# Gated cross-attention with routed experts: one copy for a head's six outputs, the exponentials' bias on GpSimd, and the row maxima one more unit ahead

## The chip, the cores and the metric

The kernel runs on one core of a Trainium2 chip. The metric is the device time of one launch in microseconds. Before the change it is 1069.77 us (median of three runs, 1069.75 to 1071.2).

## What is computed

The reference is one transformer block on 800 tokens of width 512. It has a cross-attention of 16 heads of width 32 with quantised queries, keys, values and probabilities, a gated residual, and a mixture of experts behind it. The change touches only the attention:

```python
q, k = _fq_sym(q, axis=-1), _fq_sym(k, axis=-1)      # integers times a step per row
v = _fq_sym(v, axis=2)                               # step per column
attn = softmax(einsum('bhqd,bhkd->bhqk', q, k))      # 2888 keys
attn = _fq_unsigned(attn, axis=-1)                   # x / (row max / 255), rounded, 0..255
out  = einsum('bhqk,bhkd->bhqd', attn, v)            # then the output projection
```

A row's largest probability becomes 255. So the kernel writes exp(step * s - step * max(s) + ln 255) straight as an unsigned byte, and needs the row's maximum before the first exponential.

## The kernel before, in words

The attention loop works on NTILE = 100 units. A unit is 128 query rows of one head against all 2888 keys. The 800 tokens make T = 7 row tiles, and the seventh holds 32 tokens. A head has six units of whole tiles, and four heads share a seventh, the tail unit, so each of the NG = 4 groups has GT = 25 units, the tail unit last. `tile_place(n)` gives group, head and tile of a unit.

The scores of a unit are six blocks of 481 or 482 columns (`BLOCK_W`). TensorE makes them twice, because PSUM does not hold them until the maximum is known.

- For the maximum (`for_max`, L587, products at L577): four spans per unit (`MAX_SPANS`), of two blocks, one, two and one. The spans of two blocks always use banks 0 and 1, and the others bank 2 (`MAX_BANK`). Span c waits until VectorE has reduced span c-2 (`pe.wait_ge(s_max, c - 1)`).
- For the exponentials (`for_exp`, L599, same L577): three spans of two blocks (`EXP_SPANS`) in two alternating pairs of banks. Span c waits for exponential c-2.

Each engine runs its own list in order:

- VectorE (L1056 to L1078): maximum 0 of unit n (L1052), the row maximum of unit n-1 over its four spans (L1062), maximum 1 of n, the bias of unit n-1 (L1072), maxima 2 and 3 of n. At n = 1 it also quantises the last group of values (L978 to L988). Before the loop it makes `neg_tail_step` (L1044).
- ScalarE (L884 to L891): three exponentials of unit n (L866), each followed by reading its sum; then `keep_output(n - 3)`, which copies a finished 128x32 output out of PSUM (L875). For a tail unit these are four copies (L879).
- SyncE (L449 to L460): a DMA transpose of the unit's bytes (`transpose_p`, L446). It waits for the unit's three exponentials and, as there are only NT8 = 2 target buffers, for the widening of unit n-2. Between them stand the transposing loads of keys (L401), four for each head.
- GpSimd (L1345 to L1350): widens the transposed bytes of unit n to bf16 (L1349, a 128x3072 cast) once the transpose has landed.
- TensorE (`weigh_values`, L608, L619): 24 products of the widened probabilities with the values into `OUT_BANK`, each unit behind the copy of the one before (`s_ao`).

TensorE's order is written out by hand and is what ties the rest together (L631 to L645). In pass n it issues, in turn: exponential span 0 of unit n-1, maximum span 2 of n, exponential span 1 of n-1, maximum span 3 of n, the value products of n-4, maximum span 0 of n+1, exponential span 2 of n-1, maximum span 1 of n+1.

`exp_bias`, `row_max` and `span_max` have two buffers each, by the parity of the unit.

## Time and profile before

| what | value |
|---|---|
| median of three runs | 1069.77 us |
| the profiled execution, its time | 1069.22 us |
| its span, first to last instruction | 1067.7 us (1.5 us lie around it) |
| attention loop, first to last maximum | 217 to 594 us |
| PE, DVE, ACT, POOL busy over the span | 93%, 60%, 47%, 40% |
| mean granted TensorE clock | 0.971 of full speed |

PE is TensorE, PEld its weight loads, DVE is VectorE, ACT is ScalarE, POOL is GpSimd, SP is SyncE. A busy time is a sum over instructions. A row of the time line merges instructions of one kind; "x2" in it means two instructions, and what stands in brackets is the idle time before the row and what ended it. The time of a merged row runs from its first start to its last end.

### The profile page before, as it was taken

The page shows a single profiled execution, that of the slowest core. Times are in us where ns is not written, and L with a number is a line of the kernel's source. Part 1 is how long each engine was busy: PE and PEld are TensorE (multiplying, and loading weights), DVE is VectorE, ACT ScalarE, POOL GpSimd, SP SyncE. Part 2 cuts the span into 40 slices and gives each one's busy share as a digit, 9 for nine tenths or more (in the row PEclk, how much of TensorE's full clock was granted, in tenths as well). Part 3 has the DMA queues.
Part 4 walks back from the last instruction along what each step waited for, and adds up shares of the span by engine and source line. Part 5 has one row for each costly group of instructions (what it writes and reads, how often), then busy time and mean ns, then how long its engine had stood idle before and what let it go on. Part 6 is the DMA issues. An engine that isn't in the chain of part 4 may idle for free.

```text
span 1067.7 us, 16598 instructions
## 1 busy us (share of the span) xinstructions
PE 988.1 (93%) x5718; PEld 500.9 (47%) x5719; DVE 644.1 (60%) x1140; ACT 499.1 (47%) x1072; POOL 431.7 (40%) x293
## 2 busy tenths in 40 slices
PE   5999999879999999999999699999999999999993
PEld 2334444324444444444444356555665665565551
DVE  4895766599999999999999545821111111111156
ACT  2022222259999999999999532111221122122110
POOL 1043333217777777777677500171111111111065
PEclk9999999989999999999999788999999999999996
DMA  9954655688888888888786444154445655653155
GB/s 321 226 200 178 208 192 202 195 152 146 139 139 130 141 140 143 142 138 133 133 136 111 68 168 168 39 199 141 167 176 183 230 191 188 236 181 114 49 166 152
DMA packets 268272, 172.45 MB, mean 162 GB/s; under 512 B 239344, under 2 KB 239344, under 8 KB 265904
## 3 DMA queue, kind: packets, MB, share of 16 engines
q1 hardware_dynamic: 258512, 140.14, 54.2%
q0 software_dynamic: 9696, 31.47, 8.7%
q8 instruction: 39, 0.64, 0.2%
q14 instruction: 25, 0.20, 0.1%
HBM read 68.67 MB, written 44.63 MB: 106 GB/s over the span
## 4 chain that ended last, share of the span: by engine, by line
PE 56%; DVE 16%; POOL 11%; ACT 8%; issue 6%; DMA 3%; SPq 0%; POOLq 0%; DVEq 0%; ACTq 0%
PE ps L692 17%; PE ps L712 10%; POOL arena_a L1349 8%; PE ps L577 8%; ACT arena_a L866 7%; PE ps L560 6%; PE ps L537 5%; DVE span_max L1052 4%; PE ps L619 3%; POOL expert_in L1358 2%; PE ps L662 2%; PE ps L722 1%; DVE v_q L1273 1%; PE ps L703 1%; DVE proj_i L1011 1%
## 5 line engine op out<-in xcount | busy, mean ns | idle before, releaser
L1052 DVE TENSOR_REDUCE span_max<-ps 128x1 f32<-128x481 f32 (+2 forms) x400 | 351.4, 904 | 17.5 <-PE ps L577 8.4
L866 ACT ACTIVATE arena_a<-ps,exp_bias,q_step 128x962 uint8<-128x962 f32 (+1 forms) x288 | 329.7, 1156 | 20.7 <-DVE exp_bias L1072 11.2
L1349 POOL CAST arena_a<-arena_a 128x3072 bf16<-128x3072 uint8 x100 | 273.7, 2747 | 129.3 <-DMA arena_a<-arena_a 119.0
L577 PE MATMUL ps<-arena_a,q_t 128*128 128x481 bf16 (+1 forms) x864 | 224.4, 372 | 18.6 <-DVE span_max L1052 7.0
L692 PE MATMUL ps<-arena_a,xt 128*128 x544 | 172.2, 459 | 1.7 <-issue 1.7
L1211 DVE TENSOR_TENSOR proj_d<-ps,proj_f 128x352 f32<-128x352 f32 x48 | 25.1, 524 | 205.5 <-ACT proj_f L901 205.4
L712 PE MATMUL ps<-arena_a,proj_r 128*128 (+3 forms) x288 | 134.1, 602 | 0.7 <-ACT proj_r L907 0.7
L907 ACT COPY proj_r<-ps 128x128 f32<-128x128 f32 x144 | 28.4, 270 | 227.1 <-PE ps L703 227.1
L577 PEld LDWEIGHTS ps<-arena_a,q_t 128*128 128x128 bf16 x864 | 61.5, 97 | 148.9 <-ACT arena_a L866 73.0
L692 PEld LDWEIGHTS ps<-arena_a,xt 128*128 128x128 f32 x544 | 100.4, 190 | 61.2 <-issue 17.9
L619 PEld LDWEIGHTS ps<-v_q,arena_a 128*128 128x128 bf16 x2400 | 77.0, 97 | 31.2 <-POOL arena_a L1349 12.8
L560 PE MATMUL ps<-arena_a 128*128 128x512 f32 (+1 forms) x192 | 84.5, 586 | 6.3 <-ACT xt L829 4.0
L619 PE MATMUL ps<-v_q,arena_a 128*128 128x32 bf16 (+1 forms) x2400 | 79.8, 179 | 7.6 <-POOL arena_a L1349 5.7
L537 PE MATMUL ps<-arena_a 128*128 128x512 f32 x184 | 82.2, 592 | 0.0
L1364 POOL DMA_DIRECT2D xt<-expert_in x36 | 19.4, 539 | 147.8 <-PE ps L722 145.8
L577 PE MATMUL ps<-arena_b,q_t 128*128 128x481 bf16 (+1 forms) x288 | 75.1, 370 | 3.9 <-ACT arena_a L866 0.3
L712 PEld LDWEIGHTS ps<-arena_a,proj_r 128*128 128x128 f32 (+1 forms) x288 | 52.9, 194 | 50.9 <-issue 47.0
L692 PE MATMUL ps<-arena_a,q_t 128*128 128x352 f32 x224 | 73.2, 472 | 0.0
L841 ACT CAST parts<-proj_d 128x512 bf16<-128x512 f32 x23 | 14.2, 618 | 115.8 <-DVE proj_d L1022 115.8
L1229 DVE COPY xt<-ps 128x512 f32<-128x512 f32 x34 | 23.5, 691 | 69.0 <-PE ps L712 69.0
L1358 POOL DMA_INDIRECT expert_in<-arena_b,slot_i x28 | 26.8, 959 | 89.6 <-DVE slot_i L1190 81.4
L560 PEld LDWEIGHTS ps<-arena_a 128*128 128x128 f32 x192 | 37.4, 197 | 51.8 <-issue 43.2
(166 smaller groups left out, 909.6 us busy)
## 6 DMA issues: line engine op xcount, KB each, us to landing
arena_a<-in_w_up SPq DMA_DIRECT2D x18, 1408.0 KB, 6.4
arena_a<-in_w_down SPq DMA_DIRECT2D x18, 768.0 KB, 8.4
key_parts<-parts SPq DMA_DIRECT2D x23, 512.0 KB, 2.6
expert_in<-xt SPq DMA_DIRECT2D x42, 256.0 KB, 3.0
xt<-expert_in POOLq DMA_DIRECT2D x36, 256.0 KB, 3.0
expert_out<-xt POOLq DMA_DIRECT2D x34, 256.0 KB, 2.3
arena_a<-in_ctx_t SPq DMA_DIRECT2D x3, 1536.0 KB, 13.6
expert_out<-xt SPq DMA_DIRECT2D x17, 256.0 KB, 3.1
```

What stands on the lines that cost most here:

```text
L537: last = mm(ps[:, 2 + j % 2, :], src, w_qkv[:, 0 if j < T else 1, k, :], start=(k == 0), stop=(k == DC - 1))
L560: last = mm(ps[:, 4 + v % 2, 0:w], w_qkv[:, 2, k, g * P:(g + 1) * P], ctx_sb[:, k, c * BANK:c * BANK + w], start=(k == 0), stop=(k == DC - 1))
L577: last = mm(ps[:, bank + b, 0:w], q_t[:, head, t * P:(t + 1) * P], k_t[head % NK][:, a:a + w], start=True, stop=True)
L619: last = mm(ps[:, OUT_BANK, 0:w], p_t[n % NPT][:, c, :], v_q[:, c, a:a + w], start=(c == 0), stop=(c == 2 * PC - 1))
L692: last = mm(ps[:, 1 + 2 * q + w, 0:INTER], src(k), arena_a[:, bass.ds(col + (w * DC + k) * INTER, INTER)], start=(k == 0), stop=(k == DC - 1))
L712: last = mm(ps[:, 6 + q, :], h_t[0:IW[c], q, c * P:(c + 1) * P], arena_a[0:IW[c], bass.ds(col + UPC + c * D, D)], start=(c == 0), stop=(c ...
L866: nc.scalar.activation(halves[:, :, a:a + w], ps[:, bank:bank + 2, 0:w], ACT.Exp, bias=exp_bias[:, n % 2:n % 2 + 1], scale=step_of, accum_ ...
L907: last = nc.scalar.copy(h_t[0:IW[c], q, c * P:(c + 1) * P], ps[0:IW[c], 5, c * P:(c + 1) * P])
L1052: v.tensor_reduce(span_max[:, n % 2, j:j + 1], ps[:, bank:bank + len(blocks), 0:w], AX.XY, ALU.max).then_inc(s_max, 1)
L1211: v.tensor_tensor(h_mul[:, q, 0:INTER], ps[:, 2 + 2 * q, 0:INTER], h_act[:, q, 0:INTER], ALU.mult).then_inc(s_hm, 1)
L1349: p.tensor_copy(p_t[n % NPT].rearrange("p c q -> p (c q)").rearrange("p (j i) -> p j i", j=2), pt_u8[n % NT8].rearrange("p (i j) -> p j i" ...
L1358: p.indirect_dma_start(out=expert_in, out_offset=bass.IndirectOffsetOnAxis(ap=slot_i[0:rows, j, t:t + 1], axis=0), in_=xn[0:rows, t, :], i ...
```

## The change

Four things are changed in the attention loop.

1. The outputs of the six whole units of a head go side by side into one PSUM bank (`OUT_RUNS` lists units whose outputs go together), and ScalarE copies them in one instruction of 128x192 after the sixth. A tail unit keeps its four copies. TensorE waits for a copy only at the first unit of a run.
2. The bias of the exponentials is made by GpSimd instead of VectorE. GpSimd makes those of units 0, 1 and 2 before its first widening, and then that of unit n+3 right behind the widening of unit n. A new semaphore says when `neg_tail_step` is there.
3. VectorE's row maximum of unit n-1 now waits for the bias of unit n-3, which frees its buffer. Its waits for the row maximum and for the exponentials move to GpSimd.
4. TensorE's order has the exponentials of unit n-2 and the value products of n-5 beside the maxima of n and n+1. The loop has one pass more.

```diff
+        OUT_RUNS, RUN_OF = [], []
+        for n in range(NTILE):
+            g, head, t = tile_place(n)
+            own = ("tail", g) if head is None else ("head", head)
+            if not OUT_RUNS or OUT_RUNS[-1][0] != own:
+                OUT_RUNS.append((own, []))
+            OUT_RUNS[-1][1].append(n)
+            RUN_OF.append(len(OUT_RUNS) - 1)
...
                 pe.wait_ge(s_conv, n + 1)
-                if n:
-                    pe.wait_ge(s_ao, n)
+                run = OUT_RUNS[RUN_OF[n]][1]
+                if n == run[0] and n:
+                    pe.wait_ge(s_ao, RUN_OF[n])
+                at = (n - run[0]) * HD
                 for c in range(2 * PC):
-                    last = mm(ps[:, OUT_BANK, 0:w], p_t[n % NPT][:, c, :], v_q[:, c, a:a + w],
+                    last = mm(ps[:, OUT_BANK, at:at + w], p_t[n % NPT][:, c, :], v_q[:, c, a:a + w],
...
-            for n in range(NTILE + 4):
-                if n >= 2:
-                    for_exp(n - 1, 0)
+            for n in range(NTILE + 5):
+                if n >= 3:
+                    for_exp(n - 2, 0)
                 for_max(n, 2)
-                if n >= 2:
-                    for_exp(n - 1, 1)
+                if n >= 3:
+                    for_exp(n - 2, 1)
                 for_max(n, 3)
...
-                weigh_values(n - 4)
+                weigh_values(n - 5)
                 for_max(n + 1, 0)
-                for_exp(n - 1, 2)
+                for_exp(n - 2, 2)
                 for_max(n + 1, 1)
...
             def keep_output(n):
 
+                kind, run = OUT_RUNS[RUN_OF[n]]
+                if n != run[-1]:
+                    return
                 g, head, t = tile_place(n)
                 act.wait_ge(s_av, n + 1)
-                if head is not None:
-                    last = nc.scalar.copy(attn[:, t, head * HD:(head + 1) * HD], ps[:, OUT_BANK, 0:HD])
+                src = ps[:, OUT_BANK, 0:len(run) * HD]
+                if kind[0] == "head":
+                    last = nc.scalar.copy(attn[:, 0:T - 1, head * HD:(head + 1) * HD],
+                                          src.rearrange("p (t d) -> p t d", d=HD))
...
                 if n:
                     dve.wait_ge(s_max, NM * n)
+                    if n >= 3:
+                        dve.wait_ge(s_bias, n - 2)
                     v.tensor_reduce(row_max[:, prev % 2:prev % 2 + 1], span_max[:, prev % 2, :], AX.X, ALU.max
                                     ).then_inc(s_row, 1)
                 if n < NTILE:
                     maximum(n, 1)
-                if n:
-                    g, head, t = tile_place(prev)
-                    neg_step = neg_tail_step[:, g:g + 1] if head is None else neg_q_step[:, head, t:t + 1]
-                    dve.wait_ge(s_row, n)
-                    if n >= 3:
-                        dve.wait_ge(s_exp, NE * (prev - 1))
-                    v.tensor_scalar(exp_bias[:, prev % 2:prev % 2 + 1], row_max[:, prev % 2:prev % 2 + 1],
-                                    neg_step, LOG255, ALU.mult, ALU.add).then_inc(s_bias, 1)
...
+            def bound_exps(n):
+
+                g, head, t = tile_place(n)
+                neg_step = neg_tail_step[:, g:g + 1] if head is None else neg_q_step[:, head, t:t + 1]
+                if n == 0:
+                    pool.wait_ge(s_ntail, 1)
+                pool.wait_ge(s_row, n + 1)
+                if n >= 2:
+                    pool.wait_ge(s_exp, NE * (n - 1))
+                p.tensor_scalar(exp_bias[:, n % 2:n % 2 + 1], row_max[:, n % 2:n % 2 + 1],
+                                neg_step, LOG255, ALU.mult, ALU.add).then_inc(s_bias, 1)
+
+            AHEAD = 3
+            for n in range(AHEAD):
+                bound_exps(n)
             for n in range(NTILE):
                 pool.wait_ge(s_pt[n % NT8], 16 * (n // NT8 + 1))
                 if n >= NPT:
                     pool.wait_ge(s_av, n - NPT + 1)
                 p.tensor_copy(p_t[n % NPT].rearrange("p c q -> p (c q)").rearrange("p (j i) -> p j i", j=2),
                               pt_u8[n % NT8].rearrange("p (i j) -> p j i", j=2)).then_inc(s_conv, 1)
+                if n + AHEAD < NTILE:
+                    bound_exps(n + AHEAD)
```

## Rows read from the trace of the kernel before

**Rows 1.** The page: costliest groups; form, count, busy us, mean ns, idle before.
```profile
L1349 POOL CAST arena_a<-arena_a 128x3072 bf16<-128x3072 uint8 x100 | 273.7, 2747 | 129.3 <-DMA arena_a<-arena_a 119.0
L866 ACT ACTIVATE arena_a<-ps,exp_bias,q_step 128x962 uint8<-128x962 f32 (+1 forms) x288 | 329.7, 1156 | 20.7 <-DVE exp_bias L1072 11.2
```

**Rows 2.** Stretch: PE, PEld, DVE, ACT, POOL busy (x); clock, DMA share, GB/s.
```profile
240.00:312.00 72.00, 69.16 (x727) 29.98 (x727) 69.52 (x118) 70.01 (x139) 52.87 (x21) 1.00 0.89 144
```

**Rows 3.** Time line of VectorE early in the loop, before values and copies run.
```profile
229.56 3.00 DVE L1052 TENSOR_REDUCE span_max<-ps 128x1 f32<-128x962 f32 x3
232.47 0.15 DVE L1062 TENSOR_REDUCE row_max<-span_max 128x1 f32<-128x4 f32 x1
```

**Rows 4.** Time line of VectorE, 280.3 to 289 us.
```profile
279.31 1.16 DVE L1052 TENSOR_REDUCE span_max<-ps 128x1 f32<-128x964 f32 x1
280.39 0.15 DVE L1062 TENSOR_REDUCE row_max<-span_max 128x1 f32<-128x4 f32 x1
281.02 0.20 DVE L1072 TENSOR_SCALAR exp_bias<-row_max,neg_q_step 128x1 f32<-128x1 f32 x1
281.15 3.00 DVE L1052 TENSOR_REDUCE span_max<-ps 128x1 f32<-128x962 f32 x3
284.06 0.14 DVE L1062 TENSOR_REDUCE row_max<-span_max 128x1 f32<-128x4 f32 x1
```

**Rows 5.** Time line of the weight loads of TensorE, 280.3 to 284.9 us.
```profile
280.52 0.11 PEld L577 LDWEIGHTS ps<-arena_a,q_t 128*128 128x128 bf16 x2 [0.40 <-DVE span_max L1052]
281.14 0.32 PEld L577 LDWEIGHTS ps<-arena_a,q_t 128*128 128x128 bf16 x3 [0.51 <-ACT arena_a L866]
281.57 0.85 PEld L619 LDWEIGHTS ps<-v_q,arena_a 128*128 128x128 bf16 x24
282.36 0.73 PEld L577 LDWEIGHTS ps<-arena_a,q_t 128*128 128x128 bf16 x5
```

**Rows 6.** Time line of ScalarE, 228 to 242 and 280.3 to 284.9 us.
```profile
237.01 1.16 ACT L866 ACTIVATE arena_a<-ps,exp_bias,q_step 128x964 uint8<-128x964 f32 x1 [0.16 <-DVE exp_bias L1072]
...
281.26 1.16 ACT L866 ACTIVATE arena_a<-ps,exp_bias,q_step 128x964 uint8<-128x964 f32 x1
283.53 1.16 ACT L866 ACTIVATE arena_a<-ps,exp_bias,q_step 128x962 uint8<-128x962 f32 x1
```

**Rows 7.** SyncE's transposes of the bytes (L446): from issue to landing.
```profile
DMA to landing us min/median/max: 3.6/4.0/5.4
```

**Rows 8.** Time lines of GpSimd and ScalarE around three casts.
```profile
238.05 2.75 POOL L1349 CAST arena_a<-arena_a 128x3072 bf16<-128x3072 uint8 x1 [4.14 <-DMA arena_a<-arena_a]
240.69 1.16 ACT L866 ACTIVATE arena_a<-ps,exp_bias,q_step 128x964 uint8<-128x964 f32 x1
...
361.54 2.75 POOL L1349 CAST arena_a<-arena_a 128x3072 bf16<-128x3072 uint8 x1 [1.56 <-DMA arena_a<-arena_a]
363.64 1.16 ACT L866 ACTIVATE arena_a<-ps,exp_bias,q_step 128x964 uint8<-128x964 f32 x1
...
589.83 5.44 POOL L1349 CAST arena_a<-arena_a 128x3072 bf16<-128x3072 uint8 x2 [2.16 <-DMA arena_a<-arena_a]
```

**Rows 9.** One small operation each on GpSimd and VectorE: ns min/median/max.
```profile
L1324 POOL TENSOR_SCALAR thresholds<-tile_no x1: 266/266/266, 4.8 to 4.8; 128x6 f32<-128x6 f32 x1
L1072 DVE TENSOR_SCALAR exp_bias<-row_max,neg_q_step x96: 201/203/205, 222.4 to 592.1; 128x1 f32<-128x1 f32 x96
```

**Rows 10.** ScalarE's time line at the loop's end, and a wider copy.
```profile
592.37 1.16 ACT L866 ACTIVATE arena_a<-ps,exp_bias,q_step 128x964 uint8<-128x964 f32 x1
595.85 1.18 ACT L866 ACTIVATE arena_a<-ps,exp_bias,tail_step 128x964 uint8<-128x964 f32 x1
...
L907 ACT COPY proj_r<-ps x144: 265/272/275, 666.8 to 1048.8; 128x128 f32<-128x128 f32 x96, 96x128 f32<-96x128 f32 x48
```

**Rows 11.** A tail unit: value products (weight loads), and the maximum behind them.
```profile
326.05 1.53 PEld L619 LDWEIGHTS ps<-v_q,arena_a 128*128 128x128 bf16 x24
328.20 1.16 DVE L1052 TENSOR_REDUCE span_max<-ps 128x1 f32<-128x964 f32 x1 [0.86 <-PE ps L577]
```

More of the change, by code:

```diff
@@ L289, in gated_xattn_moe_kernel @@
         s_bias = sem("exp_bias_ready")
+        s_ntail = sem("negative_tail_steps_ready")
         s_exp = sem("exp_done")
@@ L629, in _ @@
             for_exp(0, 1)
-            for n in range(NTILE + 4):
-                if n >= 2:
-                    for_exp(n - 1, 0)
+            for n in range(NTILE + 5):
+                if n >= 3:
+                    for_exp(n - 2, 0)
                 for_max(n, 2)
-                if n >= 2:
-                    for_exp(n - 1, 1)
+                if n >= 3:
+                    for_exp(n - 2, 1)
                 for_max(n, 3)
-                if n == 4:
+                if n == 5:
                     pe.wait_ge(s_vq, 16 * (NG - 1))
-                if n == (NG - 1) * GT + 4:
+                if n == (NG - 1) * GT + 5:
                     pe.wait_ge(s_vq, 16 * NG)
-                weigh_values(n - 4)
+                weigh_values(n - 5)
                 for_max(n + 1, 0)
-                for_exp(n - 1, 2)
+                for_exp(n - 2, 2)
                 for_max(n + 1, 1)
@@ L1043, in _ @@
             dve.wait_ge(s_tail, 16 * HG)
-            link(v.tensor_scalar(neg_tail_step[:, :], tail_step[:, :], -1.0, None, ALU.mult))
+            v.tensor_scalar(neg_tail_step[:, :], tail_step[:, :], -1.0, None, ALU.mult).then_inc(s_ntail, 1)
             def maximum(n, j):
@@ L1085, in _ @@
                 link(v.tensor_scalar(inv, inv, 1e-8, None, ALU.max))
-            dve.wait_ge(s_ao, NTILE)
+            dve.wait_ge(s_ao, len(OUT_RUNS))
             v.tensor_tensor(attn_tail, attn_tail, spread(tail_inv[:, :], [P, NG, HD]), ALU.mult).then_inc(s_tnorm, 1)
```

## The prediction

> **What bounds the kernel now.** I read the page first, then a stretch of the loop by engine, then the time lines of the four engines over two units, and last the path of a unit's bytes. The page names no engine as the limit of the attention loop. In the undisturbed stretch PE, DVE and ACT are each busy 96 to 97% of 72 us, and POOL 73% [rows 2]. The three full engines invite the view that each 0.2 us taken off them is 0.2 us of time. The time lines say otherwise.
>
> A unit takes 3.67 us: two row maxima stand at 280.39 and 284.06 [rows 4]. The path that repeats is this. A maximum over two banks starts at 279.31 and takes 1.16; 0.05 later, at 280.52, TensorE loads weights to refill these banks, having sat 0.40 for DVE [rows 4, 5]. At 281.15, 0.63 later, the next maximum over these banks starts [rows 4]. So one turn is 1.16 + 0.05 + 0.63 = 1.84 us, and a unit has two such spans, both in banks 0 and 1: 2 x 1.84 = 3.67 us. The second turn is alike: 281.15 + 1.16 + 0.05 = 282.36, which is when TensorE loads again [rows 4, 5]. Early in the loop no value product and no output copy runs yet. A row maximum starts 1.08 after the last two-bank maximum does (279.31 to 280.39 [rows 4]), so there the turn goes from 229.56 to 232.47 - 1.08 = 231.39, 1.83 us again [rows 3]. ScalarE, with no copy to make, waits 0.16 for its bias there and still starts its units at the pace of DVE [rows 6]. I take this turn of banks 0 and 1 as the floor. Of the 99 distances between row maxima none is under 3.67.
>
> ScalarE is as full only because it is paced. Near the end of the loop, where no maximum is left, a unit with its copy takes 595.85 - 592.37 = 3.48 us [rows 10]. In the steady stretch its first exponential starts at 281.26, 0.04 after the bias that starts at 281.02 and takes 0.20 [rows 4, 6]. That gives a second loop, as long as the first: end of a unit's exponentials, products for the next span (281.14), maximum products, 24 value products (281.57, 0.85), the refill at 282.36, maximum, row maximum, bias [rows 4, 5]. The change takes the bias out of that second loop, not out of the first.
>
> The third path is that of the bytes. Three exponentials take 283.53 + 1.16 - 281.26 = 3.43 us [rows 6]. 0.11 us or more later SyncE issues the transpose, which lands after 3.6 to 5.4, median 4.0 [rows 7]. The cast takes 2.75, and POOL waited 119.0 us in all for transposes [rows 1]. Today the cast of unit n is wanted by its value products, in the midst of the exponentials of n+3.
>
> **The change part by part.**
>
> *Copies.* 96 copies become 16 of 128x192. A copy of 128x128 takes 0.27 [rows 10], so one of 192 columns about 0.3, worked out from it. ScalarE is relieved of some 0.1 to 0.2 us a unit. It had 3.67 - 3.48 = 0.19 to spare already [rows 10], and waits for others, so I cost this at 0. The cover is the floor of 3.67; were it gone, the copies would be worth up to 0.2 x 96 = 19 us less the 16 large ones (5), about 14. Fewer waits of TensorE for copies: 0 as well.
>
> *Bias off VectorE.* 100 operations of 0.20 [rows 9] that fall, in the floor's turn, into the time in which TensorE refills banks 0 and 1. DVE from 281.02 to 281.15 has nothing else to do, since the maximum at 281.15 waits for products loaded at 280.52 [rows 4, 5]. Worth 0.
>
> *Maxima further ahead.* TensorE's order of maximum spans, their banks and waits stay. The floor stays. Exponentials lag by one pass more: the first units come one pass of 3.67 later, and behind the last maximum there are two units of exponentials where there was one, at 3.48 each [rows 10]. The same pass is counted once: +3.5 us on the path to the last value product. What hangs behind it (transpose, cast, value products, normalising) is unchanged. SyncE's key loads stand at fixed places among the byte transposes and were loaded more than a head ahead, so the unit more costs nothing there.
>
> *Bias on POOL, behind the cast.* This is the new wait. The bias of n+3 stands behind the cast of n on POOL, and the exponentials of n+3 wait for it. That closes a loop over three units: exponentials 3.43, issue 0.11, landing 4.0 (3.6 to 5.4), cast 2.75, bias, start of ScalarE 0.04 [rows 1, 6, 7]. It has 3 x 3.67 = 11.01 us. A small POOL operation of six columns takes 0.27, against 0.20 on DVE [rows 9]. With about 0.08 for two passings of semaphores (0.04 and 0.05 between DVE, ACT and PE above) I take 0.35, with 0.25 and 0.6 as ends. At the median landing the loop is 10.29 + 0.35 + 0.04 = 10.68 and fits. At the longest it is 12.1 and doesn't.
>
> How often? I took, for each n from 4 to 99, the start of unit n's exponentials less the end of the cast of n-3. The first is 240.69 - (238.05 + 2.75) = -0.11, one in the middle is 363.64 - (361.54 + 2.75) = -0.65, the last 595.85 - (589.83 + 5.44) = 0.58 [rows 8, 10]. The 96 gaps have a mean of 0.40. 40 of them are under the 0.35 that the bias would need, and together they miss 20.1 us. Each miss would hold ScalarE, and, through exponential span 1, the value products and the refill behind it, TensorE and the floor's turn too. 20.1 is the upper end: a delay at unit n also moves n+1 and n+2, whose casts don't wait for it, and slower units load the DMA engines less (share 0.89 now [rows 2]). Lower end 0: the mean gap, 0.40, is just above 0.35, so if the spread of landings evened out nothing would be lost. I take 9, near the middle, as the gaps swing from one unit to the next (-1.2 to 2.1) and a late unit can't be made up, since the floor runs at 3.67 flat. The bias also sits before the next cast: in 23 of 99 units the casts follow each other at once, and each of these is 0.3 later; that is within the 9.
>
> The Trainium skill ("GPSIMD Engine Reference", section 4.1, Engine selection, and 3.1) keeps elementwise work on VectorE, as GpSimd passes two software dispatches for an instruction and measures 1.96 times as long on two-input work. By that figure the bias would cost 0.40 and not 0.27, and the loop over three units would gain 0.13: as an estimate up to 0.13 x 96 / 3 = 4 us more. The row of the small POOL operation speaks for less.
>
> *Stalls that the unit more covers.* At a tail unit the value products take 1.53 rather than 0.85, and the maximum behind them comes 0.86 late [rows 5, 11]; at most heads' first units 0.08 is lost likewise. These add up to some 6 us over the floor. With bias in time, the exponentials would run up to 0.13 earlier against the maxima, because the third is held by TensorE's order, so 0.13 of each stall goes: about 20 x 0.08. I take -1, with 0 and -5 as ends.
>
> *Sum.* 0 + 0 + 3.5 + 9 - 1 = +11.5 on 1069.2 us of the profiled execution gives 1080.7. The median of the runs lies 0.6 above that execution, so 1081.3.
>
> **The rivals.**
>
> *A. The bytes come in time.* If landings even out, the lag of 3.5 and the relief of 1 to 2 remain: +2, 1071.8. For it: median landing gives 10.68 against 11.01. Against: 40 of 96 gaps too short.
>
> *B. Faster: the engines' own work is the limit.* If VectorE's list were the bound, 0.13 us (281.02 to 281.15) a unit go, 13 us; if ScalarE's, about 14. With the lag: 1060. It decides only if refills of banks 0 and 1 could come earlier than now; TensorE's 0.40 of waiting for DVE ahead of the refill [rows 5] says that they can't. For it speaks only the 97%.
>
> *C. The loop over three units bites in full.* The 20.1 are all paid, or the bias takes 0.5 and more behind a cast: +3.5 + 20 = 1093, and more. It needs each late cast to pass its lateness on to the next unit's transpose, through the two target buffers. For it: transposes are already issued late by the wait for the cast of n-2 in part of the units.
>
> *D. It does not do what it says.* The bias on POOL could wait for the row maximum rather than the cast. In the new order the row maximum of n is made more than a unit ahead of n's exponentials, so no; I give it nothing of its own.
>
> **How the numbers follow.** Forecast 0.62 (its own range 1074 to 1090), A 0.18, B 0.07, C 0.13. A measurement of this kernel tells about 0.2%, 2.1 us, from no change: faster is under 1067.6, slower above 1071.9. A lies at that border: 0.12 of it is no change, 0.03 a small gain, the rest slower. So faster 0.09, same 0.12, slower 0.79. The range from 1069 to 1092 leaves out B, the small gains and the upper part of C, some 0.18.
>
> **What would show it.** Right: row maxima never closer than 3.67 us; ScalarE's idle time goes up and ends on POOL's bias at L1072's successor, in about a third of the units or more; VectorE's idle time before the two-bank maxima goes up; copies and their 17 us vanish without a trace in the time; the last exponential comes 3.5 us later behind the last row maximum. Wrong: row maxima at 3.5 us (the floor was none), or ScalarE never waiting for POOL (A), or a POOL bias over 0.5 us (C).

## The result

The changed kernel takes 1086.29 us (median of four runs, 1085.43 to 1088.53), against 1069.76 us (1069.57 to 1071.2) before. The medians lie 16.5 us apart. The ratio is 1.0151, with a 95% interval of 1.0130 to 1.0172, which is 16.2 us (13.9 to 18.4). Forecast were 1081.3 us, and 1069 to 1092 as the range.

| | before | after |
|---|---|---|
| span of the profiled execution | 1067.7 us | 1084.4 us |
| its time | 1069.22 us | 1085.9 us |
| first row maximum to the last | 372.3 us | 384.9 us |
| last row maximum to the end of the last exponential | 5.2 us | 9.5 us |
| DVE, ACT, POOL busy over the span | 60%, 47%, 40% | 59%, 46%, 42% |

The page of the changed kernel, the same groups as in [rows 1] (L879 is what L866 was, L1376 what L1349 was, L1070 what L1052 was), and the table by stretches beside [rows 2]. The first line is the kernel before's own line for L1052; all others are the changed kernel's:

```profile
L1052 DVE TENSOR_REDUCE span_max<-ps 128x1 f32<-128x481 f32 (+2 forms) x400 | 351.4, 904 | 17.5 <-PE ps L577 8.4
...
L1070 DVE TENSOR_REDUCE span_max<-ps 128x1 f32<-128x481 f32 (+2 forms) x400 | 351.8, 905 | 34.0 <-PE ps L588 22.6
L879 ACT ACTIVATE arena_a<-ps,exp_bias,q_step 128x962 uint8<-128x962 f32 (+1 forms) x288 | 329.8, 1159 | 40.6 <-POOL exp_bias L1366 21.0
L1376 POOL CAST arena_a<-arena_a 128x3072 bf16<-128x3072 uint8 x100 | 274.2, 2742 | 79.4 <-DMA arena_a<-arena_a 72.6
...
240.00:312.00 72.00, 64.19 (x659) 29.15 (x659) 65.37 (x94) 64.68 (x113) 54.00 (x37) 1.00 0.84 143
```

All three full engines are less busy: PE 64.2 instead of 69.2 us in the stretch, DVE 65.4 instead of 69.5, ACT 64.7 instead of 70.0. VectorE waits 22.6 us in all for TensorE ahead of its span maxima, where it waited 8.4. ScalarE now waits 21.0 us in all for the bias that POOL makes, where it waited 11.2 for that of DVE. POOL waits less for transposes (72.6 instead of 119.0 us), but little of that is a gain. Before the change its first cast alone waited 27.97 us, and now 3.38, as the first biases stand ahead of it and do the waiting; and 100 biases take 26 us.

The operations themselves came out as estimated. Columns: ns min/median/max, first and last start, form. The indented row says who waited for the bias: ScalarE, 22.0 us in all, 22 times.

```profile
L1366 POOL TENSOR_SCALAR exp_bias<-row_max,neg_q_step x96: 264/264/268, 220.7 to 606.2; 128x1 f32<-128x1 f32 x96
  ACT arena_a L879: 22.0, 22
...
L892 ACT COPY xt<-ps x16: 306/308/319, 265.2 to 618.3; 128x192 f32<-128x192 f32 x16
```

The bias on POOL takes 0.264 us (0.27 was the estimate, from [rows 9]) and the copy of 128x192 takes 0.308 (estimate 0.3, from [rows 10]).

Here is the loop over three units at work. First POOL, then ScalarE's first exponentials, then VectorE, time lines of the changed kernel:

```profile
291.15 0.26 POOL L1366 TENSOR_SCALAR exp_bias<-row_max,neg_q_step 128x1 f32<-128x1 f32 x1
293.38 2.74 POOL L1376 CAST arena_a<-arena_a 128x3072 bf16<-128x3072 uint8 x1 [1.97 <-DMA arena_a<-arena_a]
296.22 0.26 POOL L1366 TENSOR_SCALAR exp_bias<-row_max,neg_q_step 128x1 f32<-128x1 f32 x1
296.54 2.74 POOL L1376 CAST arena_a<-arena_a 128x3072 bf16<-128x3072 uint8 x1
299.38 0.27 POOL L1366 TENSOR_SCALAR exp_bias<-row_max,neg_q_step 128x1 f32<-128x1 f32 x1
...
291.59 1.19 ACT L879 ACTIVATE arena_a<-ps,exp_bias,q_step 128x964 uint8<-128x964 f32 x1
296.51 1.16 ACT L879 ACTIVATE arena_a<-ps,exp_bias,q_step 128x964 uint8<-128x964 f32 x1 [1.20 <-POOL exp_bias L1366]
299.92 1.16 ACT L879 ACTIVATE arena_a<-ps,exp_bias,q_step 128x964 uint8<-128x964 f32 x1
...
291.07 0.15 DVE L1082 TENSOR_REDUCE row_max<-span_max 128x1 f32<-128x4 f32 x1
294.74 0.15 DVE L1082 TENSOR_REDUCE row_max<-span_max 128x1 f32<-128x4 f32 x1
298.48 0.15 DVE L1082 TENSOR_REDUCE row_max<-span_max 128x1 f32<-128x4 f32 x1
299.97 1.73 DVE L1070 TENSOR_REDUCE span_max<-ps 128x1 f32<-128x962 f32 x2 [0.68 <-PE ps L588]
303.00 0.14 DVE L1082 TENSOR_REDUCE row_max<-span_max 128x1 f32<-128x4 f32 x1
```

The cast of unit 14 starts at 293.38 and ends at 296.12. The bias of unit 17 follows 0.09 us later, and the exponentials of unit 17 start at 296.51, 0.03 after the bias ends and 4.92 us after those of unit 16. So from the end of a cast to the exponential it is 0.09 + 0.26 + 0.03 = 0.39 us (0.35 + 0.04 were taken). ScalarE then catches up with units of 3.41 and 3.55 us. The lateness reaches VectorE through TensorE's list, two passes on: 0.68 us of waiting for TensorE ahead of 299.97, and 4.52 between the row maxima at 298.48 and 303.00, where 294.74 - 291.07 = 3.67. In the whole loop 25 of the 93 units 4 to 96 start their exponentials within 0.05 us of the bias.

The lateness could also have reached VectorE straight from POOL, since the row maximum of a unit waits for the bias of two units before it, which frees its buffer. The trace rules that out: every row maximum starts 1.99 us or more after the end of that bias.

### The profile page after: what moved, and what is told of

Its sections match the earlier page's. It is cut to its first block, busy times and chain, and to the rows that moved or that the text cites. A ratio compares the mean times of both kernels' runs of the same rounds, so it can differ in the third digit from the quotient of the medians.

```text
span 1084.4 us, 16536 instructions
## 1 busy us (share of the span) xinstructions
PE 984.4 (91%) x5718; PEld 506.5 (47%) x5719; DVE 639.0 (59%) x1040; ACT 494.7 (46%) x992; POOL 458.3 (42%) x393
## 4 chain that ended last, share of the span: by engine, by line
PE 53%; DVE 14%; issue 14%; POOL 7%; DMA 7%; ACT 5%; SPq 0%; POOLq 0%; DVEq 0%; ACTq 0%
PE ps L705 17%; PE ps L725 9%; PE ps L588 7%; PE ps L571 5%; PE ps L548 5%; ACT arena_a L879 4%; DMA arena_a<-arena_a 4%; DVE span_max L1070 4%; POOL arena_a L1376 3%; PE ps L632 3%; POOL expert_in L1387 2%; PE ps L675 2%; PE ps L735 1%; DVE v_q L1285 1%; PE ps L716 1%
## 5 line engine op out<-in xcount | busy, mean ns | idle before, releaser
L1070 DVE TENSOR_REDUCE span_max<-ps 128x1 f32<-128x481 f32 (+2 forms) x400 | 351.8, 905 | 34.0 <-PE ps L588 22.6
L879 ACT ACTIVATE arena_a<-ps,exp_bias,q_step 128x962 uint8<-128x962 f32 (+1 forms) x288 | 329.8, 1159 | 40.6 <-POOL exp_bias L1366 21.0
L1376 POOL CAST arena_a<-arena_a 128x3072 bf16<-128x3072 uint8 x100 | 274.2, 2742 | 79.4 <-DMA arena_a<-arena_a 72.6
L588 PE MATMUL ps<-arena_a,q_t 128*128 128x481 bf16 (+1 forms) x864 | 219.5, 374 | 31.7 <-DVE span_max L1070 19.5
L588 PEld LDWEIGHTS ps<-arena_a,q_t 128*128 128x128 bf16 x864 | 63.9, 97 | 155.4 <-ACT arena_a L879 65.2
L854 ACT CAST parts<-proj_d 128x512 bf16<-128x512 f32 x23 | 14.2, 618 | 113.4 <-DVE proj_d L1040 113.4
L1397 POOL DMA_DIRECT2D expert_out<-xt x34 | 18.5, 545 | 106.5 <-DVE xt L1241 98.6
## 6 DMA issues: line engine op xcount, KB each, us to landing
arena_a<-in_ctx_t SPq DMA_DIRECT2D x3, 1536.0 KB, 13.4
```

The costliest lines, as they stand in the source:

```text
L588: last = mm(ps[:, bank + b, 0:w], q_t[:, head, t * P:(t + 1) * P], k_t[head % NK][:, a:a + w], start=True, stop=True)
L879: nc.scalar.activation(halves[:, :, a:a + w], ps[:, bank:bank + 2, 0:w], ACT.Exp, bias=exp_bias[:, n % 2:n % 2 + 1], scale=step_of, accum_ ...
L1070: v.tensor_reduce(span_max[:, n % 2, j:j + 1], ps[:, bank:bank + len(blocks), 0:w], AX.XY, ALU.max).then_inc(s_max, 1)
L1376: p.tensor_copy(p_t[n % NPT].rearrange("p c q -> p (c q)").rearrange("p (j i) -> p j i", j=2), pt_u8[n % NT8].rearrange("p (i j) -> p j i" ...
```

## Where the 16.5 us are

The starts of the row maxima (L1062 before; L1082 or a line nearby in the others) and the ends of the last exponential cut the loop of each profiled execution into parts. All are differences of such times in the traces, in us:

| kernel | row maxima 0 to 10 | 10 to 98 | 98 to 99 | last row maximum to the end of the exponentials | sum |
|---|---|---|---|---|---|
| before | 40.17 | 329.56 | 2.55 | 5.24 | 377.5 |
| copies alone (first experiment) | 41.93 | 329.24 | 2.54 | 5.16 | 378.9 |
| new order alone (second) | 44.44 | 327.90 | 2.55 | 8.51 | 383.4 |
| bias ahead of the cast (third) | 43.34 | 328.12 | 2.55 | 8.44 | 382.5 |
| the changed kernel | 44.27 | 337.80 | 2.80 | 9.52 | 394.4 |

The loop is 394.4 - 377.5 = 16.9 us longer in these two profiles. Each row is one execution. Outside the loop, where the kernels are alike, the time of these five varied between 690.0 and 693.1 us, so a difference of 1 or 2 us between two profiled times can come from there. The experiments that stand behind these rows follow. Every ratio is against runs of the kernel before that were made together with it.

## Experiments: one part at a time

**Copies alone.** The kernel before, with `OUT_RUNS`, the side by side outputs and the one copy of the change:

```diff
-                if n:
-                    pe.wait_ge(s_ao, n)
+                run = OUT_RUNS[RUN_OF[n]][1]
+                if n == run[0] and n:
+                    pe.wait_ge(s_ao, RUN_OF[n])
...
-                    last = nc.scalar.copy(attn[:, t, head * HD:(head + 1) * HD], ps[:, OUT_BANK, 0:HD])
...
+                    last = nc.scalar.copy(attn[:, 0:T - 1, head * HD:(head + 1) * HD],
+                                          src.rearrange("p (t d) -> p t d", d=HD))
```

> The kernel before with the first part of the change alone: a head's six outputs side by side in the bank and one copy. Theory (the turn of banks 0 and 1 is the floor, ScalarE is only paced): 1069.8 +- 1 us, the median distance of row maxima stays 3.67 us. Rival (ScalarE's 97% is the limit): 80 copies less of 0.1 to 0.2 us give 1056 to 1062. Rival (the large copy holds the next head's first value products): up to 16 x 0.15 = 2.4 us slower, 1072.

Measured: 1069.88 us, ratio 0.9999 (0.9985 to 1.0014). The median distance of row maxima is 3.68. ScalarE, freed of 80 copies, waits more for its bias instead, as the time line of its first exponentials shows:

```profile
283.57 1.16 ACT L877 ACTIVATE arena_a<-ps,exp_bias,q_step 128x964 uint8<-128x964 f32 x1
287.25 1.16 ACT L877 ACTIVATE arena_a<-ps,exp_bias,q_step 128x964 uint8<-128x964 f32 x1 [0.16 <-DVE exp_bias L1088]
291.00 1.16 ACT L877 ACTIVATE arena_a<-ps,exp_bias,q_step 128x964 uint8<-128x964 f32 x1 [0.23 <-DVE exp_bias L1088]
```

287.25 - 283.57 = 3.68, the pace of before, with 0.16 and 0.23 us of waiting where there was none behind a copy [rows 6]. 97% busy was pace, not limit.

**New order alone.** The kernel before with TensorE's order of the change; the bias stays on VectorE, its buffers are four:

```diff
-                    for_exp(n - 1, 0)
+                    for_exp(n - 2, 0)
...
-                weigh_values(n - 4)
+                weigh_values(n - 5)
...
-                    if n >= 3:
-                        dve.wait_ge(s_exp, NE * (prev - 1))
+                    if n >= 5:
+                        dve.wait_ge(s_exp, NE * (prev - 3))
```

> The kernel before with TensorE's new order alone: exponentials of n-2 and value products of n-5 beside the maxima of n. The bias stays on VectorE; its buffers are four instead of two, so that VectorE doesn't wait for exponentials. Small copies stay. Theory: the lag of one pass (+3.5 us) less the stalls that the lead covers (1 to 2) gives 1071 to 1073, row maxima never under 3.67 us apart; behind the last row maximum the exponentials end 3.5 us later than before. Rival (the order itself costs, since after the change the row maxima took 12.6 us more from first to last): 1080 to 1086.

Measured: 1074.51 us, ratio 1.0040 (1.0024 to 1.0057), 4.3 us, 1.5 us over the range expected. The stretch behind the last row maximum grew by 8.51 - 5.24 = 3.27 us, for which 3.5 was the estimate. The middle part lost 1.7 us (329.56 to 327.90; 1 was the estimate). The rest, not foreseen, is at the start and has its own experiments below.

**Bias ahead of the cast.** The changed kernel with the same operations in another order on POOL:

```diff
             for n in range(NTILE):
+                if n + AHEAD < NTILE:
+                    bound_exps(n + AHEAD)
                 pool.wait_ge(s_pt[n % NT8], 16 * (n // NT8 + 1))
...
-                if n + AHEAD < NTILE:
-                    bound_exps(n + AHEAD)
```

> The changed kernel with one move: GpSimd makes the bias of unit n+3 ahead of the widening of unit n instead of behind it. The number of its operations is the same. Theory (the loss is the loop over three units: exponentials, transpose, cast, bias): the loss beside the lag goes, 1071 to 1074, ScalarE hardly waits for the bias. Rival (the bias on GpSimd costs by itself, by its length, its semaphores or what it takes from the cast): stays at 1083 to 1087.

Measured: 1075.22 us, ratio 1.0045 (1.0028 to 1.0062), 1.2 us over the range expected. So 1.0151 - 1.0045 = 0.0106, or 11.3 us (8.4 to 14.2), hang on where the bias stands in POOL's queue. That POOL makes it costs nothing that these runs can tell: with the new order and the bias still on VectorE the ratio is 1.0040. Who waited for it, in the rows of that line:

```profile
L1366 POOL TENSOR_SCALAR exp_bias<-row_max,neg_q_step x96: 265/267/270, 219.5 to 591.4; 128x1 f32<-128x1 f32 x96
  ACT arena_a L879: 5.3, 1
```

A bias takes 0.267 here, no less than in the changed kernel, and ScalarE waits for one only once, for the first.

**One unit further.** The bias stays behind the cast, but that of n+4 behind the cast of n:

```diff
-        exp_bias = sb("exp_bias", [P, 2], f32)
+        exp_bias = sb("exp_bias", [P, 4], f32)
...
-            AHEAD = 3
+            AHEAD = 4
```

> The changed kernel with the bias still behind the cast, but one unit more ahead: behind the cast of n stands the bias of n+4 instead of n+3, with four buffers for bias and row maximum. Theory (the loop from exponentials over transpose, cast and bias closes over too few units): it now closes over four, 4 x 3.67 = 14.7 us against 10.8 + 0.4, so the loss goes as it did with the bias ahead of the cast: 1073 to 1076. Rival (the place behind the cast costs as such): 1083 to 1087.

Measured: 1076.79 us, ratio 1.0049 (1.0031 to 1.0068), 0.8 us over the range expected. The same relief by another way: the place behind the cast costs nothing as such, the loop does, and only while it closes over three units. The buffers of bias and row maximum are four here instead of two, and no run has four buffers with the bias of n+3 behind the cast. But in the changed kernel no row maximum waits for its buffer (see above), and only one bias waits for exponentials (5.1 us, once), so two buffers were not what held it.

**A longer bias.** The changed kernel with one more small operation of 0.26 us between cast and bias:

```diff
+                p.tensor_scalar(spare[:, n % 2:n % 2 + 1], row_max[:, n % 2:n % 2 + 1],
+                                neg_step, LOG255, ALU.mult, ALU.add)
                 p.tensor_scalar(exp_bias[:, n % 2:n % 2 + 1], row_max[:, n % 2:n % 2 + 1],
```

> The changed kernel with one more operation of 0.26 us on GpSimd between the cast and the bias (it writes a spare word that nothing reads). Theory: each pass of the loop over three units is 0.26 us longer; a third of the units wait today, more will then, so 4 to 9 us: 1090 to 1095. Rival (the wait for the bias is a symptom only, and something else holds the units): 1086 +- 1.5.

Measured: 1097.15 us, ratio 1.0242 (1.0215 to 1.0269). That is 0.0091 or 9.7 us (6.1 to 13.4) for 0.26 us, a little over the 4 to 9 expected (on the kernel before at 1069.8 it is 1095.7 us). Now 77 of 93 units start within 0.05 us of the bias. A loop over three units that always bound would give 0.26 x 100 / 3 = 8.7. The profiles say more: row maxima 10 to 98 take 348.05 us instead of 337.80, 10.3 more, where the loop alone could give 0.26 x 88 / 3 = 7.7. The extra operation also stands before the next cast: over units 10 to 96 a cast starts 0.36 us behind its landing on average, instead of 0.17. That is the likely rest; no run separates the two.

**Three target buffers.** The changed kernel with a third buffer for the transposed bytes (in `proj_f`, which is free in the loop):

```diff
-        NP8, NT8, NPT = 3, 2, 3
+        NP8, NT8, NPT = 3, 3, 3
```

> The changed kernel with three target buffers for the transposed bytes instead of two, so that a transpose no longer waits for the cast of two units before. Theory: the loop over three units gets shorter by the part of it that was this wait, some 0.2 us a unit on average and more in the late ones, so 4 to 8 of the 16.5 us come back: 1078 to 1082. Rival (landings alone make the late units): 1086 +- 1.5.

Measured: 1089.52 us, ratio 1.0173 (1.0149 to 1.0198). A miss: nothing came back, and against 1.0151 the two intervals overlap. Averaged over units 4 to 96, a transpose was issued 0.12 us behind the exponentials instead of 0.22, but took 4.39 us to the start of the cast instead of 4.28. 4.51 against 4.50: what the issue gained, the way to the cast took back. The wait for a buffer was no part of the loop that could be taken out. Where it went is seen in part: a cast starts 0.23 us behind its landing instead of 0.17, and the landing itself takes 4.18 instead of 4.12 (units 10 to 96). Why is not shown.

## Experiments: the floor

**Six spans over three banks.** The kernel before with the maxima in spans of one block, each refilled three spans later. The two spans more stand in TensorE's order beside the others:

```diff
-    MAX_SPANS, MAX_BANK = [[(0, 0), (1, 0)], [(0, 1)], [(0, 2), (1, 1)], [(1, 2)]], [0, 2]
+    MAX_SPANS, MAX_BANK = [[(0, 0)], [(1, 0)], [(0, 1)], [(0, 2)], [(1, 1)], [(1, 2)]], [0, 1, 2]
...
-                if c >= 2:
-                    pe.wait_ge(s_max, c - 1)
-                products(n, MAX_SPANS[j], MAX_BANK[c % 2]).then_inc(s_qa, 1)
+                if c >= 3:
+                    pe.wait_ge(s_max, c - 2)
+                products(n, MAX_SPANS[j], MAX_BANK[c % 3]).then_inc(s_qa, 1)
```

> The kernel before (bias on VectorE, no lead) with another floor: the maxima in six spans of one block over three banks, refilled three spans behind, instead of four spans over two buffers, of which two are two banks wide. VectorE's own work a unit becomes longer: six reductions at 0.57, row maximum 0.06, bias 0.13 are 3.59 us, where four are 3.48 (1.08 + 0.57 + 1.08 + 0.57 + 0.06 + 0.13). Theory (the turn of banks 0 and 1 is the floor): that turn is gone, row maxima come under 3.67 apart for the first time, 3.6 or so, and with the casts as the next limit the kernel gains 3 to 8 us: 1062 to 1067. Rival (VectorE's own work is the limit): 0.1 us a unit more, 1080.

Measured: 1064.18 us, ratio 0.9933 (0.9911 to 0.9955). VectorE's time line:

```profile
302.77 0.15 DVE L1065 TENSOR_REDUCE row_max<-span_max 128x1 f32<-128x6 f32 x1
302.83 0.65 DVE L1055 TENSOR_REDUCE span_max<-ps 128x1 f32<-128x482 f32 x1
303.40 0.20 DVE L1075 TENSOR_SCALAR exp_bias<-row_max,neg_q_step 128x1 f32<-128x1 f32 x1
303.52 2.93 DVE L1055 TENSOR_REDUCE span_max<-ps 128x1 f32<-128x481 f32 x5
306.37 0.15 DVE L1065 TENSOR_REDUCE row_max<-span_max 128x1 f32<-128x6 f32 x1
```

306.37 - 302.77 = 3.60 us, a distance under 3.67 that only the last one had before; the median is 3.58. VectorE does more work here (six reductions) and has no gap in these rows, and still it is quicker. The kernel before was held by the turn of banks 0 and 1 and not by VectorE's work.

How much that is worth in the loop is less sure than that it is so. By the ratio the kernel gains 7.2 us (4.8 to 9.5). In the one profile row maxima 10 to 98 take 326.27 us instead of 329.56, 3.3 less, where 88 distances shorter by 0.09 would give 8: 24 of them are over 3.75 us. The whole loop takes 374.8 instead of 377.5. The two profiled times differ by 4.3 us; the other 1.6 lie outside the loop, in parts that the edit does not touch.

**The same with all parts of the change**, the bias ahead of the cast and four buffers:

> The kernel with all parts of the change, the bias ahead of the cast, four buffers for bias and row maximum, and the six spans over three banks. VectorE has 3.46 us of work a unit now, ScalarE about 3.45. Theory: with the floor gone the relief of VectorE and ScalarE is worth something; the path of the bytes (two target buffers: 2 units have to hold a landing of 4.2 on average, a cast of 2.75 and the bias) limits to about 3.6: 372 us of maxima become 360 to 366, plus the lag of 3 to 4 us: 1060 to 1070. Rival (no relief is worth anything): 1074 or more.

Measured: 1070.10 us, ratio 0.9984 (0.9969 to 1.0000), the upper end of the range expected. With the floor gone the unit does get shorter: the median distance is 3.54 instead of 3.58, and early in the loop row maxima stand 3.46 apart, 0.12 less than with the bias on VectorE, where it took 0.13. The middle part of the loop takes 323.24 us instead of 326.27. But the kernel is 0.0051, 5.5 us (2.6 to 8.3), behind the six spans alone. In the profiles the stretch behind the last row maximum is 8.45 instead of 5.02 us and row maxima 0 to 10 take 42.10 instead of 40.37: the lag and the start of the new order cost more than that relief brings.

**The quickest.** Six spans, three target buffers and one copy for a head, in the order of the kernel before:

> The kernel before with the six spans over three banks, plus three target buffers for the transposed bytes and one copy for a head's six outputs. With six spans the issue of a transpose waited 0.52 us on average behind the exponentials, mostly for the cast two units before. Theory (as in the changed kernel with three buffers, the wait only moves from the issue to the landing, and copies are worth nothing): 1064 +- 1.5, no better than six spans alone. Rival (the two buffers are the limit of the six spans): 1058 to 1062.

Measured: 1062.03 us, ratio 0.9915 (0.9885 to 0.9945), so 0.9% faster than the kernel before and 2.3% than the changed one. The reading "the wait only moves" was wrong here: issue came 0.12 us behind the exponentials instead of 0.52, and the cast started 4.30 behind the issue instead of 4.38. But the two intervals overlap, so that it beats the six spans alone is likely, not shown. The profiles point the same way: row maxima 10 to 98 take 320.97 us against 326.27, though the profiled execution was the quickest of its six (1058.62 us).

## Experiments: the start

With the new order alone row maxima 6 and 7 came 5.47 and 4.40 us after the one before each, and row maxima 2 and 3 came 4.48 and 4.62 after theirs; 3.67 is the usual distance. The weight loads of TensorE in the second experiment:

```profile
246.70 0.32 PEld L577 LDWEIGHTS ps<-arena_a,q_t 128*128 128x128 bf16 x3 [0.37 <-ACT arena_a L866]
248.83 0.69 PEld L619 LDWEIGHTS ps<-v_q,arena_a 128*128 128x128 bf16 x24 [1.81 <-POOL arena_a L1349]
249.44 0.13 PEld L577 LDWEIGHTS ps<-arena_a,q_t 128*128 128x128 bf16 x2
249.83 0.15 PEld L577 LDWEIGHTS ps<-arena_a,q_t 128*128 128x128 bf16 x1 [0.25 <-issue]
250.23 0.15 PEld L577 LDWEIGHTS ps<-arena_a,q_t 128*128 128x128 bf16 x1 [0.25 <-issue]
```

Two things are to be seen: 1.81 us of waiting for the cast of unit 1, and behind it products 0.40 us apart, which is the clock's lower level (0.20 apart at the upper one). The granted clock of this profile is 0.50 from 221.9 to 235.5 us and again from 249.2 to 252.6.

**Keeping TensorE busy.** The new order alone, with 18 idle products ahead of the maxima of unit 2 and 8 ahead of the value products of unit 1:

```diff
-                pe.wait_ge(s_conv, n + 1)
                 if n:
                     pe.wait_ge(s_ao, n)
+                if n == 1:
+                    filler(8)
+                pe.wait_ge(s_conv, n + 1)
...
+                if n == 2:
+                    filler(18)
```

> The kernel with TensorE's new order alone (bias on VectorE), and 26 products that nobody reads, put where TensorE sits idle at the start of the loop: 18 ahead of the maxima of unit 2, while VectorE quantises the values (TensorE was idle 4.12 us there), and 8 ahead of the value products of unit 1 (idle 1.81 us). They run into the output bank, which is overwritten later. In the run without them eight products each from 231.9 and from 249.4 us came 0.40 apart instead of 0.20. Theory (part of what the lead costs beyond 3.5 us is TensorE's clock at the start, which falls behind the longer idle times): products 0.20 apart there, row maxima of units 2 and 3 at 3.67 us instead of 4.48 and 4.62, and the unit at 5.48 near 4: 3 us less than without them, about 1071.5. Rival (the clock is not tied to these idle times, or filling costs as much): 1074 to 1075.

Measured: 1076.68 us, ratio 1.0043 (1.0022 to 1.0064), as without them. A miss: 3 us less were expected. Its weight loads (L611 are the idle products):

```profile
228.89 0.15 PEld L611 LDWEIGHTS ps<-arena_a,q_t 128*128 128x128 bf16 x1 [0.25 <-issue]
229.28 1.73 PEld L611 LDWEIGHTS ps<-arena_a,q_t 128*128 128x128 bf16 x9 [0.23 <-issue]
246.98 1.52 PEld L611 LDWEIGHTS ps<-arena_a,q_t 128*128 128x128 bf16 x8
249.26 0.67 PEld L626 LDWEIGHTS ps<-v_q,arena_a 128*128 128x128 bf16 x24 [0.76 <-POOL arena_a L1358]
249.85 1.14 PEld L577 LDWEIGHTS ps<-arena_a,q_t 128*128 128x128 bf16 x7
```

The first fillers ran at the lower level themselves, to 229.3, and so held up unit 2 (row maxima 1 and 2 5.28 apart, then 3.67). The clock did come back sooner, at 229.3 us instead of 235.5, but nothing was won by it: row maxima 0 to 3 take 15.99 us instead of 16.13. Around the second ones the clock stayed up: the seven loads from 249.85 take 1.14 us. But row maxima 5 and 6 still stood 5.63 apart, because the cast was late all the same.

So this run doesn't separate the clock from the fillers' own time. What the profiles show is this. The granted clock fell to 0.50 between 218.5 and 222.4 us in all ten profiles of kernels with four spans. It stayed there for 6.8 us in the kernel before, and for 13.7 in the copies alone, where row maxima 2 and 3 came 4.48 and 4.62 us after theirs with the old order. So a longer stretch at the lower level, which goes with 0.8 and 0.95 us more at two row maxima, doesn't need the new order. But all seven profiles with the new order, four spans and no fillers have the longer one, and the old order has it in one of two. Whether the new order makes it more frequent stays open.

**Values later.** The new order alone, with the transpose of the last group's values out of the way of unit 1:

```diff
-                if n == 2:
+                if n == 8:
                     transpose_values(NG - 1)
```

> The kernel with TensorE's new order alone (bias on VectorE), and the DMA transpose of the last group's values issued six units later, behind the byte transpose of unit 7 instead of unit 0. It takes SyncE's queue 3.8 us, and in the new order the bytes of unit 1 wait behind it while ScalarE is already two units on; the value products of unit 1 came 1.8 us late and row maxima 6 and 7 stood 5.48 and 4.40 us apart. In the kernel before the same transpose fell into a gap. Theory: these two distances fall to 3.67 to 3.8 and the kernel takes 2 to 2.5 us less than with the new order alone, 1.0045 becomes about 1.0025 of the kernel before. Rival (the two distances come from the longer lag as such): 1.004 to 1.005 stays.

Measured: 1076.88 us, ratio 1.0058 (1.0041 to 1.0075). A miss: 1.0025 was expected. Row maxima 5 to 7 now stand 3.67 us apart, as expected, and 0 to 10 take 41.95 us instead of 44.44. But row maxima 11 to 13 stand 7.25 and 4.65 apart instead of 2 x 3.67. SyncE's time lines, first of the kernel before, then of the new order alone, then of this run:

```profile
230.39 3.76 SPq L412 DMA_TRANSPOSE v_q<-arena_b  x1
234.19 1.50 SPq L446 DMA_TRANSPOSE arena_a<-arena_a  x1
...
238.17 3.81 SPq L412 DMA_TRANSPOSE v_q<-arena_b  x1
242.03 1.50 SPq L446 DMA_TRANSPOSE arena_a<-arena_a  x1
...
260.77 4.33 SPq L412 DMA_TRANSPOSE v_q<-arena_b  x1
```

The value transpose holds SyncE's queue for 3.81 us and the bytes behind it come late: those of unit 1 are issued at 242.03, 2.9 us after their exponentials ended (239.14). In its new place it stands ahead of the bytes of unit 7 (not behind them, as the expectation has it), holds the queue for 4.33 us and makes them 4.7 us late (265.20 instead of 260.54). In the kernel before the third exponential of unit 0 ran while VectorE quantised the values and ended at 227.13; in the new order it ran behind that and ended at 234.92. So, before, the bytes of unit 0 were issued at 227.24, the value transpose right behind them at 230.39, in the gap that the quantising leaves, and the bytes of unit 1 were 1.1 us late (234.19 instead of 233.09). So the mechanism is shown, and the cure is none: 2.5 us won at one place, 4.5 lost at the other.

**Values later, in the quickest kernel:**

> The fastest kernel so far (order and bias as before the change, six spans of maxima over three banks, three target buffers for the bytes, one copy for a head) with the transpose of the last group's values six units later. Theory: there the transpose already falls into a gap, so nothing: 0.9915 +- 0.002 of the kernel before. Rival: 1 to 2 us less.

Measured: 1064.00 us, ratio 0.9938 (0.9921 to 0.9955). Row maxima 10 and 11 stand 6.82 apart there, at the place where the value transpose now stands. The step gained nothing, and its ratio lies just above the 0.9895 to 0.9935 expected. Against 0.9915 the intervals overlap.

## Why the prediction was right, and where it was off

*The copies are worth 0.* Right: 0.9999 (0.9985 to 1.0014), where they would have been worth 14 us with ScalarE as the limit.

*The bias off VectorE is worth 0, the floor is the turn of banks 0 and 1.* Right. In the changed kernel the median distance of row maxima is still 3.68; the six spans show the floor by taking it away. One sentence was wrong: of the 99 distances of the kernel before, the last is under 3.67 (2.55), as no maximum of a further unit stands in it. It bears on nothing.

*The lag costs 3.5.* Right in size: 3.27 in the new order alone, at the end of the loop.

*The bias behind the cast costs 9, between 0 and 20.* Right mechanism, somewhat under-sized. By the ratios of the two kernels that differ only in its place it is 11.3 us, with 9 inside the interval (8.4 to 14.2). By the profiles it is 12: 337.80 - 328.12 = 9.7 in the middle, 44.27 - 43.34 = 0.9 at the start and 9.52 - 8.44 = 1.1 at the end, where the last unit waits 1.04 us for its bias, and 0.25 at the last row maximum. A third of the units or more were to wait for the bias. 25 of 93 do, about a quarter: fewer than forecast, but longer each (the 26 that wait, unit 99 among them, wait 16.9 us). The count of gaps under 0.35 us (40 of 96, 20.1 us together) gave an upper end and the mean gap a lower one; the truth was just past the middle. That 9 came so near is in part luck: it was a point taken between 0 and 20.1 and not worked out. The relief hoped for from a slower pace hardly came: from the end of the exponentials to the cast it took 4.50 us against 4.60, though the DMA engines' share fell from 0.89 to 0.84.

*The relief of stalls, -1.* It was -1.7 in the middle part of the new order alone, and -1.4 with the bias ahead of the cast.

*What was missing: the start.* The order was read as one pass of lag and no more. But SyncE's queue is fixed, and the value transpose in it, hidden before, holds the bytes of unit 1 in the new order. Row maxima 6 and 7 came 5.08 and 4.57 us after those before them in the changed kernel, 2.3 us over 2 x 3.67; with the bias ahead of the cast they came 5.00 and 3.67 after, 1.3 us over. The other 1.0 goes with the place of the bias: the exponentials of unit 4 start 0.09 us behind theirs, at 247.19, after 2.60 us of waiting. The prediction looked at the key loads in that queue and not at the value transpose: a step that is moved has to be held against every entry of each queue, not only against the frequent ones.

*The sum as measured.* By the ratios 16.2 us are 11.3 for the place of the bias and 4.8 for all the rest (ratio 1.0045). In the profiles the rest is 8.44 - 5.24 = 3.2 of lag, 1.3 at row maximum 6, 329.56 - 328.12 = 1.4 of relief, and 43.34 - 40.17 - 1.3 = 1.9 at row maxima 1 to 3. Of the last, 1.6 are row maxima 2 and 3, which came late under the lower clock; the copies alone met as much (41.93 against 40.17). How often it stays low so long in either kernel isn't known from one profile each, so this part stays open. Against the forecast of 11.5 the miss of 4.7 is thus about 2.3 at the bias and 3.2 at the start, less 0.7 at lag and relief.

*The rivals.* A (the bytes come in time) fell with the 21.0 us that ScalarE waits for POOL and with the ratio of 1.0151. B (the engines' work is the limit) fell with the copies alone and the six spans. C (the loop bites in full, 1093) didn't come for this bias: 11.3 of the 20.1 us were paid. It was the better guess of the size for a bias of 0.5 us: so made, the kernel takes 1.0242, about 1095.7. D (the bias waits for the row maximum) fell too: POOL waits for a row maximum at two biases of the 100. One slip of adding: A's small gain of 0.03 and B's 0.07 make 0.10 for faster, not 0.09.

## What the runs showed of the hardware

*A small operation on GpSimd.* The same 128x1 operation takes 0.264 us on GpSimd and 0.203 on VectorE [rows 9], a factor of 1.3. The Trainium skill ("GPSIMD Engine Reference", section 3.1) measures 1.96 for a two-input operation of 2048 columns, and the prediction gave the sum by that factor as 4 us more. That is other work than this one. The measurement decides: for one column it is 1.3. Where the two engines were compared at the same place in the order, the longer operation cost nothing that the runs can tell (ratio 1.0045 on GpSimd, 1.0040 on VectorE); what cost was the place in the queue.

*TensorE's clock.* Early in the loop every profile shows the granted clock at the lower of its two levels, 1.2 GHz, where the upper is 2.4: from 220.9 to 227.7 us in the kernel before, 219.6 to 233.3 in the changed kernel, 221.9 to 235.5 in the new order alone. Products of 481 columns came 0.40 us apart there, and 0.20 elsewhere. In the new order alone TensorE's idle time of 4.12 us came at 225.6, when the clock was already low; what stood ahead of the fall were idle times of 1.1 to 1.3 us. A second fall, at 249.2 us, came right behind an idle time of 1.81. But in the changed kernel an idle time of 1.84 us, at 245.0, was followed by none. So an idle time of that length is not enough for a fall, and the run with products put into it doesn't show that they prevented one.

## What to carry to other kernels

Three engines at 96 to 97% can all be paced by a fourth thing, here one pair of banks that is filled and read in turn. Before an operation is moved off a busy engine, measure the turn: if the next piece of work there starts when another engine is done and not when its own is, the operation is free where it is.

An operation that others wait for must not stand behind one that waits for a slow transfer. Ahead of it in the same queue, or one unit further on, the same operation cost nothing that could be told here. Behind it, it cost 11.3 us, and 0.26 us more of it another 9.7.

A lead of one more unit is not free: it is paid once at the end of the loop (3.3 us), and at the start it shifts the work against every queue whose order is fixed.
